# Loads and stores of a three-level pyramid kernel on one DMA ring, half a group at a time, in turns

## The chip, the core and the metric

The kernel runs on one core of a Trainium2 chip. The time is the device time of one launch in microseconds (us). Before the change three runs gave 1297.19, 1297.73 and 1298.64 us; the median is 1297.73 us. The 1298.64 us run is the one that was profiled.

## What is computed

The input `x` is (8, 32, 512, 512) in float32. It is group-normalised over groups of two channels, a three-level low-pass pyramid replaces the top left corner of each normalised image by its smoothed and halved version, and the input is added back:

```python
def _gn(v, G=16, eps=1e-5):
    g = v.reshape(B_, G, C_ // G, H_, W_)
    m = jnp.mean(g, axis=(2, 3, 4), keepdims=True)
    s = jnp.var(g, axis=(2, 3, 4), keepdims=True)
    return ((g - m) / jnp.sqrt(s + eps)).reshape(v.shape)

def _wavelet_pyramid(x, levels=3):
    K = jnp.outer([.25, .5, .25], [.25, .5, .25])
    result = x
    for level in range(levels):
        sh, sw = H // 2 ** level, W // 2 ** level
        temp = result[:, :, :sh, :sw]                      # each channel by itself
        approx = conv(temp, K, padding='SAME')
        down = approx[:, :, ::2, ::2]
        result = result.at[:, :, :sh // 2, :sw // 2].set(down)
    return result

x = x + _wavelet_pyramid(_gn(x))
```

Every element is read once and written once: 268.44 MB in and 268.44 MB out.

## The kernel before

The unit of work is a group: two channels of 512 x 512, 2 MiB. There are 128 groups. A group lies in one of eight slots of the SBUF tensor `xs` (`SLOTS`); group n uses slot n mod 8. In a slot, a partition holds four runs of 4 KB: two channels (`c`) times the top and the bottom half of the image (`f`), each run being two neighbouring rows. The bottom half (f = 1) is only scaled and shifted. The top half (f = 0) also takes the pyramid's results. So the bottom half of a group is complete earlier than the top half.

All engines walk the groups in the same order. In step u:

- SyncE (SP) issues the load of group n as one DMA (line 144), after a wait until the store of group n - 8, the slot's last tenant, has landed (`x_stored[slot]`, line 143). The first eight loads wait for nothing.
- VectorE (DVE) makes the horizontal sums of group u (lines 305, 311, 317), then adds the level-3 corner of group u - 2 (line 292) and the level-1 result of group u - 1 (lines 277 and 280). Line 305 is the first that reads a loaded slot.
- TensorE (PE) makes the mean, the three levels and the variance with matmuls.
- ScalarE (ACT) takes the mean and the squares of group u (lines 434, 439), issues the store of group u - 2 (line 487), scales part of the top half of group u - 1 (line 473), empties level 1 from PSUM (450, 451), scales the bottom half of group u - 1 (478, which raises `scaled`) and empties level 2 (466).
- GpSimd (POOL) computes the coefficients and fixes a column.

The store of group n waits for `scaled`, `l1_added` and `l2_added` of that group. It is one DMA of 2 MiB. The last two groups are stored as four halves (line 497).

Each of the two issuing engines has its own DMA ring: loads go through SP's ring (q1 in the profile), stores through ACT's (q10). Both rings are served by the same 16 DMA engines. A DMA here is split over all 16 engines: each moves 8 partitions, 32 runs of 4 KB for a whole group, 16 for a half. The semaphore of a DMA reaches its count when all 16 have finished.

Of the kernel before, what the change touches and what calls it, by code (L numbers as in the profile page):

```python
# [14 lines left out]
HALVES = 2  # L15
RPP = 2
SLOTS = 8
LAG = 1
LAG_L3 = 2


def pyramid_kernel(nc: bass.Bass, x: bass.AP, out: bass.AP):
    B, C, H, W = x.shape
    G = B * C // CG
# [7 lines left out]
    def groups(a):  # L32
        return a.rearrange("b (g c) (f p s) w -> (b g) p (c f) (s w)", c=CG, f=HALVES, s=RPP)

    x_dram = groups(x).rearrange("(l k) p h n -> l k p h n", k=SLOTS)
    out_dram = groups(out).rearrange("(l k) p h n -> l k p h n", k=SLOTS)
    out_half = groups(out).rearrange("(l k) p (c f) n -> l k f p c n", k=SLOTS, f=HALVES)

    with ExitStack() as ctx:
# [6 lines left out]
        def sem(name):  # L46
            return ctx.enter_context(nc.semaphore(name))


        xs = sb("xs", [P, SLOTS, ROWS * W])  # L50
# [33 lines left out]
        var_ps = psum("var_ps", [P, 512])  # L84

        x_loaded = [sem(f"x_loaded{i}") for i in range(SLOTS)]
        x_stored = [sem(f"x_stored{i}") for i in range(SLOTS)]
        consts_ready = sem("consts_ready")
        const_step = sem("const_step")
        h1_part = sem("h1_part")  # L90
# [15 lines left out]
        scaled = sem("scaled")  # L106
        l1_added = sem("l1_added")
# [3 lines left out]
        l2_added = sem("l2_added")  # L111
# [3 lines left out]
        LAPS = G // SLOTS  # L115
# [3 lines left out]
        def exists(base, k):  # L119
            return not isinstance(base, int) or 0 <= base + k < G  # L120

        def later(base, k, n):
            return not isinstance(base, int) or base + k >= n
# [5 lines left out]
        def half_of(slot, f):  # L129
            return xs[:, slot, :].rearrange("p (c f n) -> p f c n", c=CG, f=HALVES)[:, f]  # L130
# [2 lines left out]
        def top_of(slot):  # L133
            return xs[:, slot, :].rearrange("p (c f s w) -> p f c s w", c=CG, f=HALVES, s=RPP)[:, 0]

        def whole(slot):
            return xs[:, slot, :].rearrange("p (h n) -> p h n", n=RPP * W)

        @block.sync
        def _(sp):  # L140
            def load(lap, slot):
                if later(lap, 0, 1):
                    sp.wait_ge(x_stored[slot], 16 * lap)
                sp.dma_start(whole(slot), x_dram[lap, slot]).then_inc(x_loaded[slot], 16)

            for lap in range(LAPS):
                for slot in range(SLOTS):
                    load(lap, slot)


            for slot in range(SLOTS):
                sp.wait_ge(x_stored[slot], 16 * (LAPS + (slot >= SLOTS - LAG_L3)))

        @block.gpsimd
        def _(pool):
# [103 lines left out]
        @block.vector  # L259
        def _(dve):  # L260
            def rstd(base, k):
                d = slice(k % 2, k % 2 + 1)
                dve.wait_ge(std_ready, base + k + 1)
                if later(base, k, 2):
                    dve.wait_ge(coef_ready, base + k - 1)
                nc.vector.reciprocal(r0[:, d], std[:, d])
                nc.vector.tensor_scalar(ve[:, d], var_ps[:, d], EPS, None, ALU.add).then_inc(r0_ready, 1)

            def add_level1(base, k):
                b = k % 2  # L270
                d = slice(b, b + 1)
                top, l1v = top_of(k % SLOTS), l1[:, b]
                dve.wait_ge(r_ready, base + k + 1)
                dve.wait_ge(l1_fixed, base + k + 1)
                for s in range(RPP):
                    right = top[:, :, s, W2:W1]
                    nc.vector.scalar_tensor_tensor(right, l1v[:, :, s, W2:W1], r[:, d], right, ALU.mult, ALU.add)  # L277
                for s in range(RPP):
                    below = top[HP:P, :, s, 0:W2]
                    last = nc.vector.scalar_tensor_tensor(below, l1v[HP:P, :, s, 0:W2], r[HP:P, d], below, ALU.mult,  # L280
                                                          ALU.add)
                last.then_inc(l1_added, 1)

            def add_corner(base, k):
                b = k % 2
                d = slice(b, b + 1)
                img = top_of(k % SLOTS)
                dve.wait_ge(l3_ps_ready, base + k + 1)
                for s in range(RPP):
                    level = l2_ps[b][HP * s:HP * (s + 1), 0:CG * W2].rearrange("p (c w) -> p c w", c=CG)  # L290
                    corner = img[0:HP, :, s, 0:W2]
                    last = nc.vector.scalar_tensor_tensor(corner, level, r[0:HP, d], corner, ALU.mult, ALU.add)  # L292
                last.then_inc(l2_added, 1)

            def step(lap, u):
                base = lap * SLOTS
                b = u % 2
                k = u - LAG
                make = exists(base, u)
                if make:  # L300
                    dve.wait_ge(x_loaded[u], 16 * (lap + 1))
                    if later(base, u, 2):
                        dve.wait_ge(l1_ps_ready, base + u - 1)
                    v = rows(u)
                    nc.vector.scalar_tensor_tensor(h1[:, b], v[:, :, 0:W:2], 2.0, v[:, :, 1:W:2], ALU.mult,  # L305
                                                   ALU.add).then_inc(h1_part, 1)
                if exists(base, k):
                    rstd(base, k)
                if make:
                    dve.wait_ge(h1_part, base + u + 1)  # L310
                    nc.vector.scalar_tensor_tensor(h1[:, b, :, 1:W1], v[:, :, 1:W - 2:2], 1.0, h1[:, b, :, 1:W1],  # L311
                                                   ALU.mult, ALU.add,
                                                   accum_out=hsum[:, b:b + 1]).then_inc(h1_ready, 1)
                    dve.wait_ge(h1_ready, base + u + 1)
                    hp = h1[:, b].rearrange("p (i s) w -> p i s w", s=RPP)
                    av = a1[:, b].rearrange("p c f w -> p (c f) w")
                    nc.vector.scalar_tensor_tensor(av, hp[:, :, 0], 2.0, hp[:, :, 1], ALU.mult,  # L317
                                                   ALU.add).then_inc(a1_ready, 1)
                if exists(base, u - LAG_L3):
                    add_corner(base, u - LAG_L3)  # L320
                if exists(base, k):
                    add_level1(base, k)

            for lap, u in HEAD:
                step(lap, u)
            with dve.Fori(1, LAPS) as lap:
                for u in range(SLOTS):
                    step(lap, u)
            rstd(G, -1)
            add_level1(G, -1)  # L330
            add_corner(G, -2)
            add_corner(G, -1)
# [92 lines left out]
        def _(act):  # L425
# [52 lines left out]
                nc.scalar.activation(bottom, bottom, ACT.Identity, bias=negmr[:, c],  # L478
                                     scale=r_plus1[:, c]).then_inc(scaled, 1)

            def store(lap, k):
                n = lap * SLOTS + k
                slot, back = k % SLOTS, k // SLOTS
                act.wait_ge(scaled, n + 1)
                act.wait_ge(l1_added, n + 1)
                act.wait_ge(l2_added, n + 1)
                nc.scalar.dma_start(out_dram[lap + back, slot], whole(slot)).then_inc(x_stored[slot], 16)


            def store_half(lap, k, f):  # L490
                n = lap * SLOTS + k
                slot, back = k % SLOTS, k // SLOTS
                act.wait_ge(scaled, n + 1)
                if f == 0:
                    act.wait_ge(l1_added, n + 1)
                    act.wait_ge(l2_added, n + 1)
                nc.scalar.dma_start(out_half[lap + back, slot, f], half_of(slot, f)).then_inc(x_stored[slot], 16)

            def step(lap, u):
                base = lap * SLOTS  # L500
                make, done = exists(base, u), exists(base, u - LAG)
                if make:
                    moments(base, u)
                if exists(base, u - LAG_L3):
                    store(lap, u - LAG_L3)
                if done:
                    scale_beside(base, u - LAG)
                if make:
                    root(base, u)
                    evacuate1(base, u)  # L510
                if done:
                    scale_bottom(base, u - LAG)
                    evacuate2(base, u - LAG)
# [3 lines left out]
            with act.Fori(1, LAPS) as lap:  # L517
                for u in range(SLOTS):
                    step(lap, u)
            store_half(LAPS, -2, 1)  # L520
            scale_beside(G, -1)
            scale_bottom(G, -1)
            store_half(LAPS, -1, 1)
            evacuate2(G, -1)
            store_half(LAPS, -2, 0)
            store_half(LAPS, -1, 0)


# [12 lines left out]
```

## Time and profile before

| What | Value |
|---|---|
| Median of three runs | 1297.73 us |
| Profiled execution | 1298.64 us, of which the span of instructions is 1296.6 us |
| PE, DVE, ACT, POOL busy | 95%, 85%, 88%, 37% of the span |
| Mean data rate of the 16 DMA engines | 414 GB/s |
| DMA engines, busy share by slice | 9 tenths or more in 39 of 40 slices |
| Granted TensorE clock, mean | 0.989 |

In the view of stretches each row is one stretch: its length, busy time and instruction count of each engine, the granted clock, the busy share of the DMA engines and the GB/s that they moved. The view of one line gives the durations of its instructions, their count, and when the first and the last of them started; for a DMA it also gives the time from its issue to its landing (minimum, median, maximum). A count such as x89 is the number of instructions in the stretch asked for.

### The profile page before, as it was taken

What the parts mean: (1) busy time and instruction counts of PE and PEld (TensorE: products, weight loads), DVE (VectorE), ACT (ScalarE), POOL (GpSimd) and SP (SyncE); (2) the same over time, 40 slices, a digit from 0 to 9 for tenths busy, and PEclk for the clock granted to TensorE, in tenths of its full rate; (3) what the DMA queues carried; (4) which work ended last, traced back from release to release, by engine and by line L of the source; (5) the groups of instructions that cost most, each with busy time, mean ns of one, the idle gap of its engine ahead of it and who ended that gap; (6) DMA issues with size and microseconds to landing.
All of it is one profiled execution on the core that took longest, in us unless ns stands there. A gap on an engine that the chain in (4) does not pass through costs nothing.

```text
span 1296.6 us, 19103 instructions
## 1 busy us (share of the span) xinstructions
PE 1236.5 (95%) x5632; PEld 705.0 (54%) x5632; DVE 1102.9 (85%) x1536; ACT 1140.2 (88%) x1282; POOL 479.2 (37%) x1316
## 2 busy tenths in 40 slices
PE   5999999999999999999999999999999999999996
PEld 2555555555555555555555555555555555555553
DVE  5888889888888888888888888888888887888874
ACT  4999999999999999999988989889898988989985
POOL 3433433433433334334343443434333343334431
PEclk9999999999999999999999999999999999999998
DMA  9999999999999999999999999999999999999996
GB/s 373 408 415 419 420 421 421 421 421 421 421 422 421 421 421 421 421 421 421 421 421 421 421 421 421 422 421 421 419 421 420 415 419 418 414 421 414 419 397 268
DMA packets 135212, 537.03 MB, mean 414 GB/s; under 512 B 4128, under 2 KB 4128, under 8 KB 135200
## 3 DMA queue, kind: packets, MB, share of 16 engines
q1 hardware_dynamic: 67584, 268.44, 50.7%
q10 hardware_dynamic: 67616, 268.44, 50.4%
q8 instruction: 5, 0.08, 0.0%
q14 instruction: 7, 0.06, 0.0%
HBM read 268.44 MB, written 268.44 MB: 414 GB/s over the span
## 4 chain that ended last, share of the span: by engine, by line
PE 41%; ACT 25%; DMA 20%; issue 9%; ACTq 2%; DVE 2%; DVEq 0%
DMA y_dram<-xs 14%; ACT xs L478 13%; PE l_ps L362 7%; PE l_ps L370 7%; DMA xs<-x_dram 7%; PE l_ps L361 6%; PE l_ps L365 6%; PE l_ps L367 6%; ACT l L451 5%; PE l_ps L398 3%; ACT squares L439 3%; ACT l L466 3%; PE var_ps L377 2%; PE l_ps L399 2%; PE l_ps L400 2%
## 5 line engine op out<-in xcount | busy, mean ns | idle before, releaser
L439 ACT ACTIVATE squares<-xs,negm 128x4096 bf16<-128x4096 f32 x128 | 474.8, 3709 | 4.2
L249 POOL TENSOR_TENSOR l<-l,col_fix 128x4 f32<-128x4 f32 x128 | 158.7, 1240 | 760.9 <-ACT l L451 760.9
L305 DVE SCALAR_TENSOR_TENSOR h<-xs 128x2048 f32<-128x2048 f32 x128 | 294.7, 2302 | 29.7 <-DMA xs<-x_dram 26.3
L311 DVE SCALAR_TENSOR_TENSOR h<-xs,h 128x2040 f32<-128x2040 f32 x128 | 291.0, 2274 | 0.0
L478 ACT ACTIVATE xs<-xs,negmr,r_plus 128x2048 f32<-128x2048 f32 x128 | 267.8, 2092 | 0.0
L292 DVE SCALAR_TENSOR_TENSOR xs<-l_ps,r,xs 64x256 f32<-64x256 f32 x256 | 123.0, 480 | 124.0 <-PE l_ps L401 122.1
L473 ACT ACTIVATE xs<-xs,negmr,r_plus 128x1024 f32<-128x1024 f32 x128 | 157.6, 1231 | 46.2 <-issue 46.1
L317 DVE SCALAR_TENSOR_TENSOR a<-h 128x1024 f32<-128x1024 f32 x128 | 157.6, 1231 | 4.4
L450 ACT ACTIVATE l<-l_ps,negm_e 128x512 f32<-128x512 f32 x128 | 87.6, 685 | 72.1 <-PE l_ps L370 72.0
L217 POOL TENSOR_TENSOR newt<-r,half_t 128x1 f32<-128x1 f32 x128 | 147.5, 1152 | 0.0
L362 PE MATMUL l_ps<-h,w_even 128*64 128x512 f32 x256 | 141.1, 633 | 0.0
L363 PE MATMUL l_ps<-h,w_prev 128*64 128x512 f32 x256 | 141.1, 633 | 0.0
L370 PE MATMUL l_ps<-a,w_odd 128*64 128x512 f32 x256 | 137.3, 618 | 0.0
L361 PE MATMUL l_ps<-h,w_prev 128*128 128x512 f32 x256 | 136.0, 614 | 0.0
L365 PE MATMUL l_ps<-a,w_even 128*64 128x512 f32 x256 | 131.9, 597 | 0.0
L366 PE MATMUL l_ps<-h,w_even 128*64 128x512 f32 x256 | 131.9, 597 | 0.0
L367 PE MATMUL l_ps<-a,w_odd 128*64 128x512 f32 x256 | 130.7, 592 | 0.0
L368 PE MATMUL l_ps<-a,w_even 128*64 128x512 f32 x256 | 130.7, 592 | 0.0
L280 DVE SCALAR_TENSOR_TENSOR xs<-l,r,xs 64x256 f32<-64x256 f32 x256 | 113.5, 484 | 1.9
L277 DVE SCALAR_TENSOR_TENSOR xs<-l,r,xs 128x256 f32<-128x256 f32 x256 | 111.0, 472 | 3.9 <-POOL r L224 3.9
L377 PEld LDWEIGHTS var_ps<-sumsq,var_w 128*128 128x128 f32 x256 | 38.1, 188 | 103.9 <-ACT squares L439 99.0
L388 PEld LDWEIGHTS l_ps<-l,w_first 128*128 128x128 f32 x256 | 38.2, 188 | 103.1 <-issue 103.0
(83 smaller groups left out, 2161.3 us busy)
## 6 DMA issues: line engine op xcount, KB each, us to landing
xs<-x_dram SPq DMA_DIRECT2D x128, 2048.0 KB, 15.1
y_dram<-xs ACTq DMA_DIRECT2D x126, 2048.0 KB, 34.7
y_dram<-xs ACTq DMA_DIRECT2D x4, 1024.0 KB, 8.7
```

The source lines that it names most:

```text
L249: nc.gpsimd.tensor_tensor(col, col, col_fix[:, b], ALU.add).then_inc(l1_fixed, 1)
L305: nc.vector.scalar_tensor_tensor(h1[:, b], v[:, :, 0:W:2], 2.0, v[:, :, 1:W:2], ALU.mult, ALU.add).then_inc(h1_part, 1)
L311: nc.vector.scalar_tensor_tensor(h1[:, b, :, 1:W1], v[:, :, 1:W - 2:2], 1.0, h1[:, b, :, 1:W1], ALU.mult, ALU.add, accum_out=hsum[:, b:b + ...
L317: nc.vector.scalar_tensor_tensor(av, hp[:, :, 0], 2.0, hp[:, :, 1], ALU.mult, ALU.add).then_inc(a1_ready, 1)
L361: nc.tensor.matmul(even, w1_prev[:], hv[:, 0, :, 1], start=True, stop=False)
L362: nc.tensor.matmul(odd_t, mid, hv[:, 0, :, 1], start=True, stop=False)
L365: nc.tensor.matmul(even_t, mid, av[:, 0], start=False, stop=True)
L367: nc.tensor.matmul(odd_t, nxt, av[:, 0], start=False, stop=True)
L370: nc.tensor.matmul(odd_b, nxt, av[:, 1], start=False, stop=True).then_inc(l1_ps_ready, 1)
L439: nc.scalar.activation(squares[:], xs[:, u % SLOTS, :], ACT.Square, bias=negm[:, b:b + 1], accum_out=sumsq[:, b:b + 1]).then_inc(sumsq_rea ...
L473: nc.scalar.activation(beside, beside, ACT.Identity, bias=negmr[:, c], scale=r_plus1[:, c])
L478: nc.scalar.activation(bottom, bottom, ACT.Identity, bias=negmr[:, c], scale=r_plus1[:, c]).then_inc(scaled, 1)
```

## The change

Loads and stores are all issued by SyncE, so there is one ring. Each is half a group: 1 MiB, 16 runs of 4 KB per DMA engine. The first eight groups are loaded in 16 halves. After that the order is: bottom of group n out, bottom of group n + 7 in, top of group n out, top of group n + 7 in, then the same with n + 1. Group 0 is stored without a load beside it. From n = 121 only stores are left, and the last two groups go bottom, bottom, top, top. A load of a half waits only for the store of the same half of the slot (`x_stored[f][slot]`), and the group counts as loaded at 32 instead of 16. ScalarE issues no DMA any more.

```diff
-    x_dram = groups(x).rearrange("(l k) p h n -> l k p h n", k=SLOTS)
-    out_dram = groups(out).rearrange("(l k) p h n -> l k p h n", k=SLOTS)
+    x_half = groups(x).rearrange("(l k) p (c f) n -> l k f p c n", k=SLOTS, f=HALVES)
     out_half = groups(out).rearrange("(l k) p (c f) n -> l k f p c n", k=SLOTS, f=HALVES)
...
-        x_stored = [sem(f"x_stored{i}") for i in range(SLOTS)]
+        x_stored = [[sem(f"x_stored{f}_{i}") for i in range(SLOTS)] for f in range(HALVES)]
...
         @block.sync
         def _(sp):
-            def load(lap, slot):
-                if later(lap, 0, 1):
-                    sp.wait_ge(x_stored[slot], 16 * lap)
-                sp.dma_start(whole(slot), x_dram[lap, slot]).then_inc(x_loaded[slot], 16)
-
-            for lap in range(LAPS):
+            def load_half(n, f):
+                lap, slot = divmod(n, SLOTS)
+                if lap:
+                    sp.wait_ge(x_stored[f][slot], 16 * lap)
+                sp.dma_start(half_of(slot, f), x_half[lap, slot, f]).then_inc(x_loaded[slot], 16)
+
+            def store_half(n, f):
+                lap, slot = divmod(n, SLOTS)
+                sp.wait_ge(scaled, n + 1)
+                if f == 0:
+                    sp.wait_ge(l1_added, n + 1)
+                    sp.wait_ge(l2_added, n + 1)
+                sp.dma_start(out_half[lap, slot, f], half_of(slot, f)).then_inc(x_stored[f][slot], 16)
+
+            for n in range(SLOTS):
+                for f in range(HALVES):
+                    load_half(n, f)
+
+            for n in range(G - LAG_L3):
+                for f in (1, 0):
+                    store_half(n, f)
+                    if 1 <= n < G - SLOTS + 1:
+                        load_half(n + SLOTS - 1, f)
+
+            store_half(G - 2, 1)
+            store_half(G - 1, 1)
+            store_half(G - 2, 0)
+            store_half(G - 1, 0)
...
-                    dve.wait_ge(x_loaded[u], 16 * (lap + 1))
+                    dve.wait_ge(x_loaded[u], 16 * HALVES * (lap + 1))
...
             def step(lap, u):
                 base = lap * SLOTS
                 make, done = exists(base, u), exists(base, u - LAG)
                 if make:
                     moments(base, u)
-                if exists(base, u - LAG_L3):
-                    store(lap, u - LAG_L3)
                 if done:
                     scale_beside(base, u - LAG)
...
-            store_half(LAPS, -2, 1)
             scale_beside(G, -1)
             scale_bottom(G, -1)
-            store_half(LAPS, -1, 1)
             evacuate2(G, -1)
-            store_half(LAPS, -2, 0)
-            store_half(LAPS, -1, 0)
```

On SyncE, from the start, the loads before stand alone in the program. A name such as x_stored0 is the semaphore of slot 0:

```order
L144 DMA xs<-x_dram 128x4x1024 x8
L144 DMA xs<-x_dram 128x4x1024 [waits x_stored0]
L144 DMA xs<-x_dram 128x4x1024 [waits x_stored1]
L144 DMA xs<-x_dram 128x4x1024 [waits x_stored2]
L144 DMA xs<-x_dram 128x4x1024 [waits x_stored3]
```

The same place after; x_stored1_0 is the bottom half of slot 0, x_stored0_0 its top half:

```order
L141 DMA xs<-x_dram 128x2x1024 x16
L150 DMA y_dram<-xs 128x2x1024 [waits scaled]
L150 DMA y_dram<-xs 128x2x1024 [waits l2_added,l1_added,scaled]
L150 DMA y_dram<-xs 128x2x1024 [waits scaled]
L141 DMA xs<-x_dram 128x2x1024 [waits x_stored1_0]
L150 DMA y_dram<-xs 128x2x1024 [waits l2_added,l1_added,scaled]
L141 DMA xs<-x_dram 128x2x1024 [waits x_stored0_0]
L150 DMA y_dram<-xs 128x2x1024 [waits scaled]
L141 DMA xs<-x_dram 128x2x1024 [waits x_stored1_1]
```

Every store now stands between loads of the same engine. The last load shown waits for x_stored1_1, the bottom half of group 1, whose store is the third store row: between the two lie a load, a store, a load and a store. From there on it is always these four.

On ScalarE, one step of the head, before:

```order
L439 ACTIVATE squares,sumsq<-xs,negm 128x4096 [waits var_ready,negm_ready]
L487 DMA y_dram<-xs 128x4x1024 [waits l2_added,l1_added,scaled]
L473 ACTIVATE xs<-xs,negmr,r_plus 128x2x2x256 [waits coef_ready]
L459 ACTIVATE std<-var_ps,eps_t 128x1 [waits r0_ready,var_ready]
L450 ACTIVATE l<-l_ps,negm_e 128x2x256 [waits l1_added,l2_ps_ready,negm_e_ready,l1_ps_ready]
```

After, the row between the squares and the scaling is gone:

```order
L456 ACTIVATE squares,sumsq<-xs,negm 128x4096
L490 ACTIVATE xs<-xs,negmr,r_plus 128x2x2x256
L476 ACTIVATE std<-var_ps,eps_t 128x1
L467 ACTIVATE l<-l_ps,negm_e 128x2x256
```

Nothing else moves on ScalarE, and nothing at all on TensorE, VectorE and GpSimd.

## Rows read from the trace of the kernel before

**Rows 1.** The page: busy shares, DMA by slice, rings.

```profile
PE 1236.5 (95%) x5632; PEld 705.0 (54%) x5632; DVE 1102.9 (85%) x1536; ACT 1140.2 (88%) x1282; POOL 479.2 (37%) x1316
DMA  9999999999999999999999999999999999999996
GB/s 373 408 415 419 420 421 421 421 421 421 421 422 421 421 421 421 421 421 421 421 421 421 421 421 421 422 421 421 419 421 420 415 419 418 414 421 414 419 397 268
q1 hardware_dynamic: 67584, 268.44, 50.7%
q10 hardware_dynamic: 67616, 268.44, 50.4%
```

**Rows 2.** Waits: who, for what; us in total, times, longest us.

```profile
SPq L144 <- DMA y_dram<-xs: 1176.9, 120, 25.2
...
ACT xs L473 <- issue: 46.1, 37, 2.8
...
DVE h L305 <- DMA xs<-x_dram: 26.3, 25, 9.0
```

**Rows 3.** Line 144 (load issues), from 205 to 1100 us.

```profile
L144 SPq DMA_DIRECT2D xs<-x_dram x89: 367/368/368, 209.8 to 1097.5; - x89
...
DMA to landing us min/median/max: 15.0/15.1/15.9
```

**Rows 4.** Line 305 (first reader of a slot), 35 to 600 and 1240 to 1290 us.

```profile
L305 DVE SCALAR_TENSOR_TENSOR h<-xs x59: 2293/2308/2327, 38.5 to 599.9; 128x2048 f32<-128x2048 f32 x59
...
L305 DVE SCALAR_TENSOR_TENSOR h<-xs x3: 2297/2302/2327, 1245.0 to 1265.1; 128x2048 f32<-128x2048 f32 x3
```

**Rows 5.** Line 487 (store issues) from 36 to 60, then from 700 to 1200 us.

```profile
L487 ACTq DMA_DIRECT2D y_dram<-xs x3: 378/378/429, 36.9 to 56.2; - x3
...
DMA to landing us min/median/max: 10.4/14.0/14.5
...
DMA to landing us min/median/max: 34.5/36.3/37.9
```

**Rows 6.** Stretches (columns as described above), one ring working, then both, then one.

```profile
4.00:8.50 4.50, 0.00 (x0) 0.00 (x0) 0.00 (x0) 0.00 (x0) 3.08 (x13) 1.00 1.02 418
15.00:36.90 21.90, 19.64 (x72) 8.62 (x72) 14.66 (x19) 18.82 (x22) 8.05 (x22) 0.92 1.03 410
200.00:600.00 400.00, 394.51 (x1819) 225.17 (x1820) 355.49 (x499) 368.14 (x412) 148.38 (x415) 1.00 1.02 421
1266.00:1269.00 3.00, 3.00 (x12) 1.91 (x13) 2.99 (x4) 2.26 (x5) 0.25 (x1) 1.00 1.01 406
1270.50:1273.30 2.80, 2.67 (x15) 1.59 (x16) 1.81 (x4) 2.77 (x5) 1.84 (x8) 1.00 0.07 26
1288.00:1290.00 2.00, 0.00 (x0) 0.00 (x0) 0.00 (x0) 0.00 (x0) 0.00 (x0) 0.51 1.03 406
```

**Rows 7.** Line 144 from 0 to 30 us, and from 1240 us.

```profile
L144 SPq DMA_DIRECT2D xs<-x_dram x8: 427/4056/5190, 0.8 to 20.8; - x8
...
  DVE h L305: 9.0, 1
...
L144 SPq DMA_DIRECT2D xs<-x_dram x1: 368/368/368, 1248.3 to 1248.3; - x1
...
DMA to landing us min/median/max: 15.0/15.0/15.0
```

**Rows 8.** DVE in order of time: last additions to groups 0, 1 and 127.

```profile
35.81 0.97 DVE L292 SCALAR_TENSOR_TENSOR xs<-l_ps,r,xs 64x256 f32<-64x256 f32 x2 [1.81 <-PE l_ps L401]
...
45.48 0.98 DVE L292 SCALAR_TENSOR_TENSOR xs<-l_ps,r,xs 64x256 f32<-64x256 f32 x2 [0.97 <-PE l_ps L401]
...
1286.13 0.97 DVE L292 SCALAR_TENSOR_TENSOR xs<-l_ps,r,xs 64x256 f32<-64x256 f32 x2 [1.60 <-PE l_ps L401]
```

More of the change, by code:

```diff
@@ L134, in top_of @@
             return xs[:, slot, :].rearrange("p (c f s w) -> p f c s w", c=CG, f=HALVES, s=RPP)[:, 0]
-        def whole(slot):
-            return xs[:, slot, :].rearrange("p (h n) -> p h n", n=RPP * W)
         @block.sync
         def _(sp):
-            def load(lap, slot):
-                if later(lap, 0, 1):
-                    sp.wait_ge(x_stored[slot], 16 * lap)
-                sp.dma_start(whole(slot), x_dram[lap, slot]).then_inc(x_loaded[slot], 16)
-            for lap in range(LAPS):
+            def load_half(n, f):
[22 more added lines that the diff above has]
+            store_half(G - 1, 0)
+            for f in range(HALVES):
                 for slot in range(SLOTS):
-                    load(lap, slot)
-            for slot in range(SLOTS):
-                sp.wait_ge(x_stored[slot], 16 * (LAPS + (slot >= SLOTS - LAG_L3)))
+                    sp.wait_ge(x_stored[f][slot], 16 * LAPS)
         @block.gpsimd
@@ L479, in scale_bottom @@
                                      scale=r_plus1[:, c]).then_inc(scaled, 1)
[L481 to L497, printed above, removed]
             def step(lap, u):
```

## The prediction, made before the changed kernel was run

> **What bounds the kernel now.** I read the page first, then the waits, then the issue times of loads and of their first reader, then stretches of the data rate. The page shows two candidates side by side [rows 1]: PE is busy 95% of the span, and the DMA engines sit at 9 tenths or more in 39 of 40 slices, with 421 GB/s on the plateau. A busy share does not settle it, so I compare two periods. Where the computation has data enough, line 305 starts 59 times from 38.5 to 599.9 us: (599.9 - 38.5) / 58 = 9.68 us per group [rows 4]. The loads are issued 89 times from 209.8 to 1097.5 us: 887.7 / 88 = 10.09 us per group [rows 3]. The transfers are the slower by 0.41 us. The computation starts with eight loaded slots, eats this lead, and then waits in small pieces: line 305 waited 25 times, 26.3 us in all, 9.0 of them the very first load [rows 2]. SP waited 1176.9 us for stores to land [rows 2], so a load starts when a slot comes free, never later. The DMA path bounds.
>
> One more thing is in these rows. A group moves 2 x 2.097 = 4.194 MB, and 4.194 MB in 10.09 us is 416 GB/s, while the engines moved 421 in the same part of the run [rows 6]. And at the end, from 1270.5 to 1273.3 us, 26 GB/s still flowed, which is one sixteenth of 421 [rows 6]. So one DMA engine of the 16 lags behind the others, and since a semaphore needs all 16, its pace is the kernel's. Stores show the backlog grow: from issue to landing 14.0 us at first, 36.3 us in the later part [rows 5]. This is inferred from rates; no row names the engine.
>
> **The change part by part.**
>
> *ScalarE without DMA issues.* 126 + 4 issues leave ACT's queue. What they cost it is at most the time that line 473 waited for nothing shown, 46.1 us in 37 times [rows 2]. It lies beside transfers that take longer (9.68 against 10.09 us), so I take it at 0. It would count only if transfers fell under 9.68 us per group; then it could be worth some part of 46.1 us. A loss is excluded, since nothing is added to ACT.
>
> *SyncE as the only issuer.* 512 issues at about 0.37 us [rows 3] are 4 x 0.37 = 1.5 us per group on a queue that otherwise only waits: 0.
>
> *Stores now stand in line with loads.* What is queued behind a waiting store is every later load, and DVE's line 305 waits for those. The store of the top of group 1 is the first that could block: its data is ready at 45.48 + 0.98 = 46.5 us [rows 8], and store 0 at 35.81 + 0.97 = 36.8. In one ring at 5.12 us per 2 MiB (below) the eight loads end at 9.0 + 7 x 5.12 = 44.8, store 0 at 49.9, and the top of group 1 is reached 5.1 us later, at 55.0. It is ready 8.5 us earlier, and this slack grows by the difference of the two periods. Cost 0; if the cover were gone, the floor would be the computation's 9.68 us per group, still under the ring's.
>
> *The load's wait.* A half's load waits for the store of the same half, with four transfers between them in the ring: 4 x 2.56 = 10.2 us of queued work. A lone transfer's pipeline delay is 9.0 - 0.8 - 5.1 = 3.1 us at the start [rows 7], so the ring stays fed: 0. But the other 15 engines can now be no more than those 10.2 us ahead of the slowest.
>
> *Halves in place of wholes.* 512 completions instead of 258. The stretch from 15.0 to 36.9 us crosses four boundaries between loads at 410 GB/s, and from 1288 to 1290 us halves of stores follow each other at 406, like the wholes at 1266 to 1269 [rows 6]. I take 0.
>
> *One ring in place of two.* This is the term that decides. Before shows one ring alone only with transfers of one direction: 418 GB/s for loads while no engine computes (4.0 to 8.5 us), 410 once they compute (15.0 to 36.9), 406 for stores (1266 to 1269). Both rings together reach 421 beside the same computation [rows 6]. What is unknown is whether 421 comes from there being two rings to pick from, or from reads and writes being mixed. The new ring alternates in runs of 16 packets per engine, not packet by packet. Bounds per group: 4.194 / 0.421 = 9.96 us, if the mixing alone gives it and no engine lags; 4.194 / 0.406 = 10.33 us at the stores' pace. I take 410, the longest stretch of one ring beside computation and nearest to what each run of 16 packets meets: 10.23 us, 2.097 / 0.410 = 5.115 us per 2 MiB.
>
> *The sum.* The ring never runs empty, so 256 times 2 MiB go through it in a row. The first has landed at 9.0 us [rows 7], the others follow: 255 x 5.115 = 1304.3. Span 1313.3 us. The computation does not lengthen this: load 127 is the 249th transfer and lands at 9.0 + 248 x 5.115 = 1277.5; line 305 of the last group started at 1265.1 and the last addition ended at 1286.13 + 0.97 = 1287.1 [rows 4, 8], so 22.0 us later, now 1299.5. The ring reaches the last half at 1310.7, 11 us after it is ready. Before, the span is 1296.6 of 1298.64 us, 2.0 around it: 1315.3 for a profiled execution. That execution was 0.9 above the median of its three runs: 1314.4, so 1315 as forecast.
>
> A rule against this sum: the Trainium skill, "DMA: Bandwidth & Descriptors", section "Issuing engines are not separate DMA queues", says that it makes no difference to the bandwidth which engine starts a DMA, since all run on the same 16 engines. By it the change of ring costs nothing, and the time is that of the rival "nothing changes" below. The rows agree so far as both rings share one total, but 410 against 421 in rows 6 is a difference that it does not foresee. The same page's section "Bandwidth" gives 341 GB/s for a 1 MB transfer, 78% of peak; by it a group would take 4.194 / 0.341 = 12.3 us, an estimate from that page. The halves at 406 GB/s behind each other in rows 6 contradict it for queued transfers.
>
> **The rivals.** With one lap of loads (44.8 us), store 0 (5.1), 120 groups at period P, and seven stores (35.8), the span is 85.7 + 120 P. P = 10.23 gives 1313.3 again.
>
> *Faster: the mixture keeps 421 and the laggard goes.* P = 9.96 gives 1280.9, and 1282 as a median. Place: the 120 groups with both directions; price: 0.13 us per group. For it: 16 engines did move 421 GB/s for 400 us beside the computation, one ring without computation reached 418, and in one ring the engines are held within 10.2 us of each other, so a lag of 36.3 - 14.0 = 22 us [rows 5] cannot build up. Against it: the only rows of one ring beside computation are 410 and 406, and holding the engines together does not speed up the slow one. It decides from P under about 10.07. The computation allows it: from group 3 at 38.5 us, 124 x 9.68 later is 1238.8, and 22.0 more is 1260.8.
>
> *Nothing changes.* The slow engine keeps its pace of the mixture: P = 10.09 gives 1296.5, and 1298 as a median. For it: the laggard's pace already is the kernel's. Against: again 410 beside 421.
>
> *Slower still: each change of direction costs something.* Four changes a group, 480 in all; 0.05 us each is 24 us, 1339 in all. No row has two directions in one ring. The 3.1 us that an empty pipeline costs would be 1488 us and is the other bound; queued transfers of one direction follow without a visible gap, so I keep only the low part, up to 0.1 us.
>
> **How the numbers follow.** The forecast (P from 10.15 to 10.33; 1304 to 1326) has 0.52. Faster with 421 (1275 to 1292) 0.25. Nothing changes (1290 to 1303) 0.15. Direction changes that cost (over 1326) 0.08. About 0.2%, 2.6 us, is what a measurement can tell from no change, so "same" is 1295.1 to 1300.3. Of "nothing changes" about half lies there, the rest is split to both sides, somewhat more to slower: faster 0.28, same 0.08, slower 0.64. The range 1281 to 1326 leaves out about 0.1 below and 0.1 above; the likeliest case alone spans 1304 to 1326.
>
> **What would show it.** In the profile after: loads spaced 10.15 to 10.33 us per group; a plateau near 410 GB/s instead of 421; all DMA in one ring; longer waits of line 305 for loads in the later part, since the computation keeps 9.68 us until its lead is gone, about group 57 (9.68 against 10.23 us eats 31 us); SP waiting for stores to land, not for `scaled` or `l2_added`; the last load landing near 1277 and line 305 of group 127 starting then. Wrong would be: a plateau at 420 or more with load spacing under 10.07 (the faster rival); slices with the DMA share under 9 in the middle (a ring that runs empty); or stores at the head of the ring that wait for ACT or DVE.

## The result, and the profile after

The changed kernel takes 1353.03 us in the median of four runs (1347.49 to 1358.89). The kernel before took 1298.18 us beside it. The ratio is 1.0426, 95% interval 1.0409 to 1.0443: 4% slower. The forecast was 1315, slower, and its range ended at 1326. So the sign was right, but the time was outside the range. A ratio here compares only runs within 1.5% of the fastest run of their kernel.

The page of the changed kernel, first the span, then busy shares, data rate by slice and the ring:

```profile
span 1355.7 us, 19119 instructions
PE 1252.3 (92%) x5632; PEld 706.5 (52%) x5632; DVE 1101.4 (81%) x1536; ACT 1141.7 (84%) x1282; POOL 610.1 (45%) x1316
DMA  9999999999999999999999999999999999999997
GB/s 379 415 419 420 420 420 421 421 421 420 421 421 419 412 366 378 417 417 416 357 334 371 420 418 415 416 412 362 355 352 348 371 415 417 416 354 343 405 419 325
q1 hardware_dynamic: 139264, 536.90, 101.0%
```

Against [rows 1] the plateau is the same, 421 GB/s, not the 410 that the sum took. But in four places the rate falls to 334 to 378 for several slices. The DMA engines are nearly as busy there as elsewhere. So each packet takes longer; the engines are not simply without work. Worked out from the packets of the trace: the mean 4 KB packet took 159 ns from 200 to 400 us and 190 ns from 650 to 720 us, and most of the excess lies in packets of 0.3 to 1.3 us.

Stretches of the same kernel (columns as in [rows 6]), a good one, then slow ones and a good one between them:

```profile
200.00:400.00 200.00, 197.22 (x907) 112.37 (x906) 178.62 (x249) 183.75 (x207) 73.34 (x201) 1.00 1.03 421
500.00:590.00 90.00, 85.91 (x397) 49.14 (x396) 77.37 (x109) 79.73 (x91) 41.74 (x87) 1.00 1.01 395
660.00:665.00 5.00, 4.36 (x27) 2.58 (x26) 4.71 (x8) 4.21 (x5) 4.49 (x9) 1.00 0.97 290
650.00:740.00 90.00, 79.78 (x335) 43.65 (x334) 64.67 (x92) 67.90 (x76) 43.91 (x77) 0.92 0.99 349
750.00:850.00 100.00, 94.62 (x439) 54.38 (x438) 85.03 (x120) 88.11 (x99) 53.33 (x100) 1.00 1.02 417
900.00:1060.00 160.00, 143.27 (x610) 78.22 (x610) 119.24 (x166) 123.42 (x140) 80.20 (x140) 0.94 1.00 360
```

The granted clock falls to 0.92 in the slow stretch from 650 us, and in the good ones it is 1.00. From 500 to 590 us the rate is down to 395 at a clock of 1.00, so a lower clock is not needed for a slow stretch. The computation is starved: line 322 (305 before) now waits for loads 75 times, 141.8 us in all, against 26.3 in [rows 2].

The waits of the changed kernel, VectorE's and then SP's:

```profile
DVE h L322 <- DMA xs<-x_dram: 141.8, 75, 8.6
...
SPq L141 <- DMA y_dram<-xs: 999.7, 240, 6.3
SPq L150 <- ACT xs L495: 47.7, 23, 6.7
...
SPq L149 <- DVE xs L309: 5.7, 6, 2.1
```

All 240 loads that have a store to wait for do wait for it, and stores wait little for the computation. Nor do their waits lie where the slow stretches are: of the 53.4 us, 1.1 fall between 480 and 1275 us. The load issues from 200 to 400 us stand here against [rows 3]:

```profile
L141 SPq DMA_DIRECT2D xs<-x_dram x39: 379/380/380, 204.2 to 396.2; - x39
...
DMA to landing us min/median/max: 11.2/12.5/12.6
```

(396.2 - 204.2) / 38 = 5.05 us per half, 10.11 per group; before it was 10.09. In a slow stretch SP's issues in order of time are:

```profile
659.23 0.38 SPq L141 DMA_DIRECT2D xs<-x_dram  x1
659.72 0.41 SPq L150 DMA_DIRECT2D y_dram<-xs  x1
664.29 0.38 SPq L141 DMA_DIRECT2D xs<-x_dram  x1
664.72 0.77 SPq L150 DMA_DIRECT2D y_dram<-xs  x1
670.87 0.38 SPq L141 DMA_DIRECT2D xs<-x_dram  x1
671.36 0.41 SPq L150 DMA_DIRECT2D y_dram<-xs  x1
675.93 0.38 SPq L141 DMA_DIRECT2D xs<-x_dram  x1
676.36 0.65 SPq L150 DMA_DIRECT2D y_dram<-xs  x1
682.95 0.38 SPq L141 DMA_DIRECT2D xs<-x_dram  x1
```

The steps are 5.06, 6.58, 5.06 and 7.02 us: every second pair is late, by 1.5 to 2 us. From the landings of all loads (each load's 16 completions are in the trace), the spacing per group is 9.96 to 10.6 us nearly everywhere, and over 10.6 in 37 groups, which together exceed 10.11 by 54.7 us. With P = 10.11 the prediction's own form gives 85.7 + 120 x 10.11 = 1298.9, and with 54.7 it is 1353.6, against a span of 1355.7. So the loss is these 37 groups.

Two more things come from the completions and packets. The tables are worked out: the lag is the time from the 15th to the 16th engine's completion of a group's store (in the changed kernel of its bottom half), and P is the time from the landing of the store before to this one's. The longer slow stretches begin at group 43 or 44 with a lag of 5.1 to 5.8 us, then at groups 58, 84 and 108 with 5.7 to 6.4:

```
group                      12    24    36    48    57    60    63    72    78    90
lag, changed kernel, us   0.6   2.4   4.0   5.0   6.2   8.5   8.3   5.3   6.0   6.5
P, changed kernel, us    10.6  10.1  10.1  10.8  10.1  11.8  12.3  10.1  10.1  12.1

group                      16    32    48    64    80    96   120
lag, before, us           0.9   5.4   9.7  14.1  19.5  23.1  22.1
P, before, us            10.2  10.1  10.1  10.1  10.1  10.1  10.0
```

The stores' lag grows by 0.14 us per group in the changed kernel and by 0.28 before. Before, the lag of the loads stays near 1 us, so the arrears stand in the ring of the stores alone.

And packets that took over 1.3 us instead of 159 ns: none from 200 to 450 us, none from 590 to 650 us, 19 from 650 to 720 us. The kernel before has none from 200 to 1250 us.

### The profile page after: what moved, and what is told of

Same layout as the page of the kernel before. It is cut to its first block, busy times and chain, and to the rows that moved or that the text cites. A ratio compares the mean times of both kernels' runs of the same rounds, so it can differ in the third digit from the quotient of the medians.

```text
span 1355.7 us, 19119 instructions
## 1 busy us (share of the span) xinstructions
PE 1252.3 (92%) x5632; PEld 706.5 (52%) x5632; DVE 1101.4 (81%) x1536; ACT 1141.7 (84%) x1282; POOL 610.1 (45%) x1316
## 4 chain that ended last, share of the span: by engine, by line
DMA 61%; PE 22%; ACT 11%; issue 3%; SPq 1%; DVE 1%; ACTq 0%; DVEq 0%
DMA y_dram<-xs 58%; ACT xs L495 6%; PE l_ps L387 4%; PE l_ps L379 4%; PE l_ps L378 3%; PE l_ps L382 3%; PE l_ps L384 3%; DMA xs<-x_dram 2%; ACT l L468 2%; PE l_ps L415 2%; SPq L141 1%; ACT l L483 1%; PE var_ps L394 1%; PE l_ps L416 1%; PE l_ps L417 1%
## 5 line engine op out<-in xcount | busy, mean ns | idle before, releaser
L266 POOL TENSOR_TENSOR l<-l,col_fix 128x4 f32<-128x4 f32 x128 | 148.2, 1158 | 675.3 <-ACT l L468 675.3
L322 DVE SCALAR_TENSOR_TENSOR h<-xs 128x2048 f32<-128x2048 f32 x128 | 294.7, 2302 | 143.5 <-DMA xs<-x_dram 141.8
L379 PE MATMUL l_ps<-h,w_even 128*64 128x512 f32 x256 | 147.1, 658 | 0.0
L380 PE MATMUL l_ps<-h,w_prev 128*64 128x512 f32 x256 | 147.1, 658 | 0.0
L378 PE MATMUL l_ps<-h,w_prev 128*128 128x512 f32 x256 | 140.3, 632 | 0.0
L383 PE MATMUL l_ps<-h,w_even 128*64 128x512 f32 x256 | 134.0, 605 | 0.0
L233 POOL TENSOR_TENSOR newt<-r 128x1 f32<-128x1 f32 x128 | 119.6, 934 | 9.2 <-DVE ve L284 7.4
L365 PE MATMUL mean_ps<-hsum,mean_w 128*128 128x1 f32 x256 | 48.5, 259 | 64.1 <-DVE h L328 63.9
L234 POOL TENSOR_TENSOR newt<-r,half_t 128x1 f32<-128x1 f32 x128 | 100.5, 785 | 0.0
```

Of the source, the lines that this page charges most:

```text
L266: nc.gpsimd.tensor_tensor(col, col, col_fix[:, b], ALU.add).then_inc(l1_fixed, 1)
L378: nc.tensor.matmul(even, w1_prev[:], hv[:, 0, :, 1], start=True, stop=False)
L379: nc.tensor.matmul(odd_t, mid, hv[:, 0, :, 1], start=True, stop=False)
```

## The experiments

Two theories were set against each other first. Theory A: one DMA engine lags. In one ring the others can be ahead of it only by what is queued before SP must wait (for a store to land, or for the computation). When that room is used up, the 15 run dry and start again together, and this disturbs the transfers. Theory B: changes of direction, or the many completions, cost time by themselves.

**e1: more room before the load's wait.**

```diff
-                    if 1 <= n < G - SLOTS + 1:
-                        load_half(n + SLOTS - 1, f)
+                    if 2 <= n < G - SLOTS + 2:
+                        load_half(n + SLOTS - 2, f)
```

> One ring and halves as in the changed kernel, but the load beside the store of group n is group n + 6, not n + 7, so it waits for the store of group n - 2: eight transfers (20.5 us of queue) lie between a half's store and the load that waits for it, not four (10.2 us). Theory A (short lead: one DMA engine lags 3 to 9 us, the load waits for it, the 15 others run dry and restart together in slow bursts): the lag finds room, the stretches at 350 GB/s vanish, 10.1 us per group all through, 1297 to 1304 us. Theory B (changes of direction or the many completions in one ring cost time by themselves): their number is the same, so 1345 to 1359 us as in the changed kernel.

Measured: 1320.5 us median, single runs 1305.31, 1312.73, 1328.27 and 1347.74. The profiled one (1312.73) by slice:

```profile
GB/s 380 395 419 420 419 421 420 421 421 421 421 420 420 420 421 420 421 420 421 421 419 410 418 414 405 419 417 416 405 400 419 419 411 418 418 415 389 373 383 275
```

In this run the slow stretch comes only at 1180 us, seven groups are over 10.6, and the lag reaches 9.3 us in good stretches, not 6. That gain is what A says, but it is not reliable: the slowest run lies among those of the changed kernel (1347.49 to 1358.89). SP's waits:

```profile
SPq L150 <- ACT xs L495: 174.1, 57, 6.7
SPq L149 <- DVE xs L309: 42.2, 29, 2.1
```

No load waits for a store any more. Stores now wait for ScalarE and VectorE, but mostly early: 189.0 of these 216.3 us lie before 600 us, and 2.3 between 600 and 1200 us. What holds SP there is the issuing itself. The load issues from 600 to 1150 us:

```profile
L141 SPq DMA_DIRECT2D xs<-x_dram x109: 2327/2555/5162, 596.8 to 1145.4; - x109
...
SPq L150 <- ACT xs L495: 2.1, 12, 0.2
```

An issue that took 379 ns in the changed kernel takes 2555 ns, and by issues and landings six or seven halves are under way on the slowest engine when one ends. The kernel before shows the same for its stores from 700 to 1200 us, with four whole groups under way:

```profile
L487 ACTq DMA_DIRECT2D y_dram<-xs x50: 383/1588/4652, 699.3 to 1191.6; - x50
```

So the ring itself seems to hold only so much, and this bounds the room in e1, not the distance of eight transfers.

**e2: less room.** The load is issued ahead of the store in each pair.

```diff
-                    store_half(n, f)
                     if 1 <= n < G - SLOTS + 1:
                         load_half(n + SLOTS - 1, f)
+                    store_half(n, f)
```

> As the changed kernel, but within each pair the load is issued ahead of the store, which leaves two transfers (5.1 us) between a half's store and the load that waits for it. Same number of halves and of changes of direction. Theory A: less room than a lag of 3 us needs, so the engines run dry in all groups and not in a third of them: over 1400 us. Theory B: 1345 to 1359 us.

Measured: 1391.14 us median of 1369.13 to 1411.47; ratio to before 1.0587 (1.0537 to 1.0638).

```profile
GB/s 380 367 347 370 361 409 421 421 421 416 415 398 348 395 418 418 416 369 363 402 396 361 351 357 382 365 354 366 409 366 348 347 346 353 405 408 362 352 372 388
```

The slices are those of the 1411.47 us run. It is slow from the second slice on, with 75 groups over 10.6, and the lag seldom passes 1.3 us. With the same transfers and changes of direction, the fastest run is 10 us longer than the slowest of the changed kernel, so B alone can't be right. The median did not reach the "over 1400", nor were all groups slow.

**e3: whole groups on one ring**, same order, same bytes between a store and its load.

```diff
-                for f in (1, 0):
-                    store_half(n, f)
-                    if 1 <= n < G - SLOTS + 1:
-                        load_half(n + SLOTS - 1, f)
+                store(n)
+                if 1 <= n < G - SLOTS + 1:
+                    load(n + SLOTS - 1)
```

> One ring, the order and the lead of the changed kernel, but whole groups of 2 MiB (the last two stored as halves): half the changes of direction and half the completions. Between a store and the load that waits for it lie two whole transfers, 10.2 us as in the changed kernel. Theory A: same room, so slow stretches again, 1330 to 1370 us. Theory B: half of the 55 us goes, 1320 to 1330 us.

Measured: 1306.23 us (1304.54 to 1312.79), ratio 1.007 (1.0045 to 1.0094). Both numbers missed.

```profile
GB/s 376 410 413 415 419 421 421 421 421 421 421 421 421 420 413 417 414 416 415 420 415 408 416 419 414 410 397 412 400 409 401 414 401 402 395 408 415 417 419 332
```

The lag grows to 4 or 5 us and stays there, as a room of 10.2 us allows. But the rate falls only to 395, and five groups pass 10.6. So A is incomplete: the same 10.2 us of room goes with 55 us of loss with halves in turns, and with 8 us with wholes. Of all runs this is the closest comparison, but a store here also waits until its whole group is computed.

**e4: halves on two rings.** Loads and stores as before, each issued as two halves with their own semaphores.

> Two rings as before the change, but every group is loaded and stored in two halves, each with its own semaphore. Theory A: the store ring holds a backlog of some 35 us as before, so nothing runs dry: 1296 to 1302 us. Theory B, in the form that completions of halves cost time: 20 us or more over before.

Measured: 1307.09 us (1306.60 to 1312.05), ratio 1.0077 (1.0054 to 1.0100). Neither: halves cost 9 us with two rings, in dips to about 395 GB/s from 800 us on. That is a sixth of the loss.

**e5: both halves of a store, then both halves of a load**, on one ring.

```diff
                 for f in (1, 0):
                     store_half(n, f)
-                    if 1 <= n < G - SLOTS + 1:
-                        load_half(n + SLOTS - 1, f)
+                if 1 <= n < G - SLOTS + 1:
+                    for f in (1, 0):
+                        load_half(n + SLOTS - 1, f)
```

> As the changed kernel (one ring, halves, the same number of completions), but both halves of a store are issued, then both halves of a load: half as many changes of direction, and five transfers (12.8 us) instead of four between a half's store and its load. If the number of directions changes or of separate waits makes the difference between the whole groups on one ring (1306 us) and the halves (1353 us), 1304 to 1315 us. If the size of a transfer makes it, 1340 to 1360 us.

Measured: 1305.75 us, four runs within 0.07 us of each other, ratio 1.0061 (1.0045 to 1.0078).

```profile
GB/s 378 413 416 420 418 420 421 420 421 420 420 421 420 421 420 417 414 412 414 414 414 407 415 414 416 414 417 411 403 420 415 415 417 411 417 416 406 409 418 297
```

The number and size of the transfers are the changed kernel's, and 47 us of its 55 are gone. The lag still meets its ceiling (about 7 us), but the excess of groups over 10.6 is 3.3 us in place of 54.7. So neither the size of a DMA nor the number of completions alone makes the loss. The turns are now of 2 MiB, as in e3, but the room has grown as well, to five transfers (12.8 us). e3 had the turns of 2 MiB at the old room of four, and e1 a larger room with turns of 1 MiB, with runs up to 1348 us. Together they point to the turns of 1 MiB; no run changes the turns alone.

**e6 and e7: the transfers alone.** All engines but the issuing ones do nothing, and a store waits for `x_loaded` of its group.

> All computing is left out: x is copied to the output in the order and with the transfers of the changed kernel, a store waits only for its group to be loaded. Theory A (a lagging DMA engine and a short lead, nothing of the compute engines): the lag and stretches at 350 GB/s are there too, 1320 to 1355 us. Rival C (the compute engines' reads and writes of SBUF slow one DMA engine): no lag, no slow stretch, near 421 GB/s all through, 1280 to 1290 us.

> All computing is left out: x is copied with the two rings and whole groups of the kernel before. Theory A: one DMA engine lags here too, 10.08 us per group, 1293 to 1298 us. Rival C: no lag, 9.95 us per group, 1278 to 1285 us.

Measured: 1284.59 us (1284.47 to 1284.97) in the changed order, 1280.98 us (1280.89 to 1281.07) in the order before. By slice, e6 and then e7:

```profile
GB/s 379 416 421 421 421 421 421 421 421 421 421 421 421 421 421 421 421 421 421 421 421 421 421 421 421 421 421 421 421 421 421 421 421 421 421 421 421 421 421 371
```

```profile
GB/s 369 422 421 422 422 421 422 422 421 422 422 421 422 422 421 422 422 421 422 422 421 422 421 421 422 422 421 422 422 421 422 422 421 422 422 421 422 422 421 404
```

Rival C is right that the computation is needed: without it there is next to no lag (2.4 us at the end of e6, 0.1 in e7) and no slow stretch, with all changes of direction and completions in place. The median spacing of loads is 9.96 and 9.95 us. When nothing computes, the whole price of one ring in halves by turns is 3.6 us.

**e8: which engine lags.** Ten tiny loads on ScalarE's ring at the end of the kernel before, of k partitions each.

> The kernel before, with ten tiny loads (k partitions, one 64-byte run each, k = 15, 14, 13, 12, 10, 8, 6, 4, 2, 1) put into ScalarE's ring behind the store of group 125, where the other engines are 6 us ahead of the lagging one. A load of k partitions runs on k DMA engines. If the laggard is outside these k, the load lands with the 15 others near 1280 us; if it is among them, near 1286 us. So the largest k that lands early names it. The time of the kernel itself should move by less than 8 us.

Measured: 1299.69 us. Last completion of each load, worked out from the trace:

```
partitions = DMA engines used      15      14      13      12      10       8       6       4       2       1
last completion, us           1285.84 1286.04 1286.24 1286.43 1286.61 1286.80 1286.99 1283.68 1283.85 1284.11
```

With 6 engines the load still waits for the laggard, with 4 it does not. The trace has k completions for each (and one earlier update at its issue), so k engines work on it. Which k they are, it does not show: if they are the first k, the laggard is the fifth or sixth.

**e9 to e11: what makes it lag.** The copy of e7 with one kind of work beside it.

> The copy with two rings and no computing (1281 us, no lag), and beside it TensorE alone, which runs the kernel's matmuls of all 128 groups on zeroed tiles, waiting for nothing, in a loop whose body is eight steps (352 matmuls with their weight loads), as in the real kernel. Theory F (the lagging DMA engine also brings TensorE's instructions each time round the loop): the lag grows by about 0.14 us per group, up to 1293 us if the matmuls run as long as the copy. If the lag comes from VectorE and ScalarE using SBUF: no lag, 1281 us.

> The same matmuls in a loop whose body is two steps, 64 times round. Theory F: a shorter body needs fewer instructions brought, if it stays where it is between two rounds, so little or no lag, about 1281 us. If TensorE's use of SBUF made the lag, the same time as with the long body.

> The copy with two rings, and beside it VectorE and ScalarE at work on tiles of their own in SBUF for some 8 us in every 10, with few instructions; TensorE does nothing. If their use of SBUF slows one DMA engine: a lag that grows by about 0.14 us per group and 1290 us or more. Theory F: no lag, 1281 us.

Measured: 1287.8, 1287.22 and 1282.45 us, one run each. The lag at group 120 is 4.8, 5.4 and 1.3 us. TensorE's work alone makes one engine lag, by 0.04 us per group, about a third of the 0.14 in the full kernel (10.09 against the 9.95 of e7). The length of its loop makes next to no difference, so Theory F falls. VectorE and ScalarE at work for 69% and 70% of the span, with few instructions, leave a lag of 0.01 us per group, so their use of SBUF is not the main cause.

**e12: less room on the computation's side.**

```diff
-                    if 1 <= n < G - SLOTS + 1:
-                        load_half(n + SLOTS - 1, f)
+                    if 3 <= n < G - SLOTS + 3:
+                        load_half(n + SLOTS - 3, f)
```

> As the changed kernel, but the load beside the store of group n is group n + 5. From a half's store to the load that waits for it there are now twelve transfers (30 us), but from a group's load to its store only three groups of traffic (30 us), and the computation needs about 27 us from a landing to the store (two steps of 9.68 us and 7 us). Theory A (the ring runs dry on the 15 faster engines as soon as their lead over the slow one exceeds the smaller of the two rooms): nothing is left for a lead, slow from the start, over 1380 us, with SP waiting for ScalarE and VectorE. Rival D (only the room between store and load counts): no worse than the 1320 us of lead 6.

Measured: 1364.69 us median, single runs 1331.75 to 1395.53.

```profile
GB/s 380 337 411 419 420 420 421 421 420 420 421 421 420 421 420 421 421 421 421 420 375 356 361 359 376 358 385 362 374 362 381 361 376 412 420 419 405 408 419 267
```

There is three times the distance between store and load, and yet it is slower than e1: 1331.75 us is the fastest run, against 1305.31. SP's waits are only for ScalarE (179.2 us) and VectorE (46.7 us), but in the slow stretch they are nearly absent, and again the issues take long. The load issues from 680 to 1100 us:

```profile
L141 SPq DMA_DIRECT2D xs<-x_dram x74: 2664/3022/6954, 681.5 to 1095.5; - x74
```

So a slow stretch needs neither a load that waits for a store nor a store that waits for the computation. The ring's own limit stood in the way of both theories: Rival D's added distance could not be used, and A's number failed, as the kernel ran well up to group 63 with a lag of 8.5 us. Why e12 is slower than e1 is open.

**e13: fewer, larger matmuls.** As e9, with 9 matmuls of 512 columns per group in the program, 18 in the trace.

```diff
+                for i in range(9):
+                    nc.tensor.matmul(l1_ps[b][:, i % 2], w[:], hv[:, 0, :, 1], start=True, stop=True)
```

> The copy with two rings and TensorE alone at work for as long as in e9, but with 18 matmul instructions of 512 columns per group instead of 44 mixed ones. If the lag of one DMA engine goes with the number of instructions: about 2 us at the end (5 us in e9). If it goes with TensorE's busy time or the data it reads: 5 us or more.

Measured: 1282.47 us, and the lag at group 120 is 0.9 us. The pages of e9 and then of e13:

```profile
PE 1202.3 (93%) x5632; PEld 689.7 (54%) x5632; POOL 11.4 (1%) x13
```

```profile
PE 991.7 (77%) x2304; PEld 438.7 (34%) x2304; POOL 11.4 (1%) x13
```

41% of the instructions in 82% of the busy time leave about a fifth of the lag. At group 96, with TensorE still at work in both, it is 1.0 against 5.0 us. So TensorE's busy time does not set it. The number of instructions fits better, but 0.9 is under the 2 us expected by it, and the matmuls also differ in shape and tiles, so that cause is not shown.

## Why the prediction was wrong

**What bounds the kernel: right.** The transfers, and among them one engine that lags. e6 and e7 show the pace without it, 9.96 us per group. For e8 the laggard is among six engines and not among four. That the lag comes from the computation I did not see.

**One ring in place of two: the term was mis-sized.** I took 10.23 us per group from stretches with one direction only. One ring with both directions moves 421 GB/s beside the computation, and P is 10.11. So the mixture of reads and writes over the 16 engines reaches 421 with one ring as with two. The term is worth 120 x (10.11 - 10.09) = 2.4 us, not 17. So the sign of the forecast came out right by luck: its reason, 410 GB/s, did not hold, and with P = 10.11 the sum gives 1298.9 for the span, next to no change. Here the rule of the Trainium skill ("DMA: Bandwidth & Descriptors", "Issuing engines are not separate DMA queues"), that the issuing engine makes no difference to the bandwidth, was nearer than my rows: 1284.59 against 1280.98 us without computation. The 341 GB/s that the Trainium skill gives on that page, section "Bandwidth", for a 1 MB transfer does not hold for the queued ones here: 421.

**The load's wait and halves in place of wholes: the step that failed.** The sum let 256 times 2 MiB pass at one pace, because both these terms stood at 0. Measured, 37 groups ran slow and cost 54.7 us. For the halves I had looked only at boundaries between transfers of one direction ("I take 0"). In one ring at the same room, wholes in their place take 1306.23 us and not 1353.03 (e3), so in turns of 1 MiB beside the computation they are worth some 47 us. The load's wait I priced at 0 with "the ring stays fed", and went on to say that the 15 engines can be no more than 10.2 us ahead of the slowest. I drew no price from that second sentence, though [rows 5] showed a backlog grown by 22 us. Half the room costs at least 10 us more (e2), so this is no 0 either. How the 54.7 us divide between the two is open, and e12 has such stretches with no load waiting. The lag came to 5 or 6 us, not 10.2, when slow stretches began. From about 400 us on the first engine completes a store half some 7.5 us after its issue, and from 200 to 300 us it was about 10 (medians, worked out from the trace), so by then less is queued on the fast engines. The sign that I had set for an empty ring, slices with a DMA share under 9, did not show: only the last slice is under 9, while the rate falls to 334 GB/s.

**Slower still, the rival with 0.08, named the right side, but a price for each change does not fit.** Without computation a group with four changes of direction takes 9.96 us (e6), and in the good stretches of the changed kernel 10.11. The loss comes in some groups only, and e2 has more of it with the same changes. That the changes play a part beside the computation is not excluded: e3 and e5 have half as many. Its sum of up to 0.1 us per change would have reached 1363.

**The end.** The ring's order puts seven stores behind the last load, as the sum has it. In e5, with few slow groups, line 305's successor starts the last group at 1267.9 us, 2.8 us later than before, and the span is 7.4 us longer. So of the 59.1 us between the two spans, 7.4 are what one ring costs even in e5 (2.4 of them pace and 3.3 its own slow groups), and nearly all the rest the slow groups: 51.7 us between the spans of e5 and the changed kernel.

**ScalarE, SyncE, stores in line:** priced at 0, and nothing in the trace contradicts this for the changed kernel. SP waited 53 us for the computation in 29 places, nearly all before the first slow stretch and after the last. In e1 and e12 the issues themselves became long, 2.6 and 3.0 us in the median for a load in place of the 0.37 I had counted.

**What is shown and what is not.** Shown: the loss is in groups whose packets take longer, and it needs both the computation beside the transfers (1353 with it, 1285 without) and halves in turns (1353, against 1306 with wholes or grouped). The lag at which slow stretches begin moves with the order: under 1.3 us mostly in e2, 5 to 6 in the changed kernel, 8.4 and 9.3 in e12 and e1. Not shown: that the 15 engines run dry and that their restart does the harm. A lag at its ceiling is not enough for it, since e3, e5 and most of e1 ran at theirs with few slow groups. Also open is why turns twice as long prevent it, and whether TensorE alone beside the changed order would bring it about, which was not run. The long packets go with the slow groups, but no run isolates them. What in TensorE's instructions reaches a DMA engine is open, and also what makes the other two thirds of the lag. No version tried beats the kernel before.

## What to carry to other kernels

If a semaphore needs all 16 DMA engines, plot the time from the 15th to the 16th completion over the run: a lag of 1% is invisible in busy shares. Where one queue carries loads and stores, give both rooms a price: store to the load that reuses its slot, and load to its own store. Look at the duration of the issuing instructions too: where 0.38 us becomes 2 or more, more distance in the program adds nothing. And try whole transfers or longer turns per direction before alternating small ones. A mean rate from stretches with one direction says little about a mixture.

## What the hardware did that I had not expected

- One DMA engine of 16 (the fifth or sixth, if a load of k partitions uses the first k) falls behind by 0.14 us in 10.09 while the engines compute. It does so by 0.04 with TensorE alone, about 0.01 with VectorE and ScalarE alone, and by no more than 0.4 us in the whole run with neither (e7).
- With TensorE alone the lag at group 120 is 4.8 us for 44 matmul instructions per group and 0.9 us for 18 larger ones.
- In a slow stretch the DMA engines count as busy (share 0.97 at 290 GB/s). Their busy share can't tell work from stalled packets.
- An issuing instruction takes 0.38 us in the median of the changed kernel's loads, with four to six halves under way. It takes 1.6 us for the late stores of the kernel before, with four whole groups under way, and 2.6 and 3.0 us for the loads of e1 and e12, with six to seven halves.
- Runs of one kernel then scatter: 1347 to 1359, 1305 to 1348 and 1332 to 1396 us in the changed kernel, e1 and e12, against 0.07 us in e5.
